# Sorting edges by source in a graph kernel: ranks from pairs of columns, a marked maximum, run sums turned afterwards, and the sort's preparation dealt out over the dense front

## The reference

```python
h = relu(layernorm(x))
feat = (h @ W).reshape(N, 2, 64); el, er = (feat*attn_l).sum(-1), (feat*attn_r).sum(-1)
e = leaky_relu(el[src] + er[dst]);  alpha = softmax of e over the edges of each dst
x = x + layernorm(segment_sum(feat[src]*alpha, dst) + bias)*gamma + beta
agg = h = relu(layernorm(x))
for _ in range(3):
    t = agg[dst]                                     # tail = dst, head = src
    att = ((agg[src] @ q_w) * tanh(rel * t @ k_w)).sum(1)
    w = softmax of att over the edges of each src
    agg = normalise(segment_sum(w * rel * t, src) / max(cnt, 1)); out += agg + h
```

## Time and profile before

| | |
|---|---|
| median of 3 runs | 9688.9 us (9686.51 to 9689.91) |
| the profiled execution | 9688.46 us, span 9686.6 us |
| mean granted clock of PE | 0.966 |
| front, from the first feature product to the first rank | 30.9 to 69.6 us |
| sort, first rank to last run sum | 69.6 to 778.9 us |
| start of the attention loop | about 850 us |

### The profile page before, as it was taken

One profiled execution on the slowest core, in us unless ns is written; L12 is line 12 of the kernel. 1 busy time (PEld: TensorE's weight loads), 2 busy tenths in 40 slices (PEclk: granted clock), 3 DMA queues, 4 the chain that ended last, 5 costly groups with the idle time before them and its releaser, 6 DMA issues.

```text
span 9686.6 us, 277606 instructions
## 1 busy us (share of the span) xinstructions
PE 8121.7 (84%) x65693; PEld 7065.2 (73%) x65693; DVE 7856.9 (81%) x33661; ACT 7227.1 (75%) x23594; POOL 6824.5 (70%) x7069
## 2 busy tenths in 40 slices
PE   7996777777775888888887888888887888888887
PEld 6985666666664777777776777777776777777776
DVE  7998999999997777777777777777776777777777
ACT  2204999999997777777776777777776777777777
POOL 1335777777775777777776777777776777777776
PEclk9998999999998999999998999999998999999998
DMA  2002444444444555555555555555555555555555
GB/s 53 5 12 77 109 107 109 107 109 109 109 108 115 158 159 160 157 157 158 160 159 163 158 159 160 157 157 159 160 158 162 158 159 160 158 157 158 160 159 146
DMA packets 1133287, 1309.57 MB, mean 135 GB/s; under 512 B 452805, under 2 KB 846875, under 8 KB 1132861
## 3 DMA queue, kind: packets, MB, share of 16 engines
q1 hardware_dynamic: 902182, 843.26, 28.5%
q0 software_dynamic: 229264, 460.98, 18.8%
q10 hardware_dynamic: 1670, 3.16, 0.1%
HBM read 1041.61 MB, written 261.38 MB: 135 GB/s over the span
## 4 chain that ended last, share of the span: by engine, by line
PE 35%; DMA 21%; issue 16%; DVE 11%; POOL 11%; ACT 3%; SPq 1%; DVEq 1%; POOLq 0%; ACTq 0%
PE bank L770 28%; DMA agg<-agg_d,arena 18%; POOL agg L732 11%; PE bank L930 2%; PE bank L915 2%; PE bank L883 2%; DMA agg<-feat_d,arena 2%; DVE arena L1709 2%; DVE agg L1610 2%; DVE agg L1600 2%; ACT arena L1045 1%; ACT arena L1125 1%; DVE arena L1686 1%; DVE arena L1590 1%; DVE arena L1684 1%
## 5 line engine op out<-in xcount | busy, mean ns | idle before, releaser
L732 POOL DMA_INDIRECT agg<-agg_d,arena x5124 | 4871.4, 951 | 1684.9 <-issue 1378.8
L1709 DVE TENSOR_TENSOR arena<-agg,bank 128x256 f32<-128x256 f32 x2562 | 1079.1, 421 | 1392.4 <-DMA agg<-agg_d,arena 1175.6
L770 PE MATMUL bank<-arena 128*128 128x129 f32 x10248 | 1760.4, 295 | 317.5 <-ACT arena L1125 294.1
L732 POOL DMA_INDIRECT agg<-feat_d,arena x1708 | 1618.0, 947 | 532.0 <-issue 410.1
L770 PEld LDWEIGHTS bank<-arena 128*128 128x128 f32 x10248 | 1377.5, 195 | 445.5 <-issue 435.2
L1121 ACT ACTIVATE arena<-arena 128x1 f32<-128x1 f32 x2562 | 755.1, 295 | 1167.9 <-DVE arena L1574 1146.6
L770 PE MATMUL bank<-tmp,wide 128*128 128x256 f32 x5124 | 1577.3, 391 | 4.8 <-DMA wide<-left_d 4.8
L770 PE MATMUL bank<-tmp,kw_s 128*128 128x256 f32 x5124 | 1567.0, 388 | 0.1
L930 PE MATMUL bank<-ident,arena 128*128 128x128 f32 x5124 | 1026.7, 283 | 508.4 <-DVE arena L1709 505.8
L930 PEld LDWEIGHTS bank<-ident,arena 128*128 128x128 f32 x5124 | 694.5, 144 | 931.7 <-DVE arena L1709 711.6
L1116 ACT ACTIVATE arena<-agg,arena 128x256 f32<-128x256 f32 x2562 | 1341.6, 524 | 16.8 <-DVE arena L1702 11.9
(11 more groups left out here) (244 smaller groups left out, 17334.3 us busy)
## 6 DMA issues: line engine op xcount, KB each, us to landing
state_d<-arena SPq DMA_DIRECT2D x488, 455.0 KB
arena<-key_d SPq DMA_DIRECT2D x489, 448.0 KB
arena<-type_d SPq DMA_DIRECT2D x367, 448.0 KB
wide<-left_d SPq DMA_DIRECT2D x2562, 64.0 KB
agg<-agg_d,arena POOLq DMA_INDIRECT x5124
agg<-feat_d,arena POOLq DMA_INDIRECT x1708
arena<-er_d SPq DMA_DIRECT2D x854, 1.0 KB
arena<-peers SPq DMA_DIRECT2D x489, 7.0 KB
```

The costliest lines, as they stand in the source:

```text
L732: nc.gpsimd.indirect_dma_start(out=rows_r[:, k % R, c, 0:width], out_offset=None, in_=table, in_offset=bass.IndirectOffsetOnAxis(ap=peer_r ...
L770: return nc.tensor.matmul(out, lhsT, rhs, start=start, stop=stop)
L1709: V.tensor_tensor(val_r[:, j % R, :, 0:F], rows_r[:, j % R, :, 0:F], bank[0][:, 0:G].rearrange("p (c f) -> p c f", c=2), ALU.mult).then_in ...
```

## The change

Seven edits, made together:

1. The seven passes and `spread(0)`, `carry(0)` are no longer ahead of the feature copies; `fields(t)` deals them out between the steps.
2. `couple` is the sum of `block_hot` over pairs of neighbouring columns (DVE, bf16, 6 x 49). Rank adds pairs instead of single columns; the column before an odd one is added by one matmul with a step of two.
3. Rank adds also 4096 on the own block (`mark16`, a diagonal). The slot is then the maximum over blocks, taken straight from the bank, and slot_hot compares with 4096 to 4159.
4. `gather_runs` has `slot_hot` as weights (64 columns) and both halves of `carried` (98 columns) moving, into 64 partitions; ACT copies the sums (`summed`) and PE transposes them a turn later (`turn_runs`), before ACT makes the run.
5. Three of 13 columns of `carried` are made by ACT (`carry_share`, six activations), the rest by DVE.
6. `run_at` has four places; DVE waits for the store of run n-4.
7. `er` is stored as node, block x head, and loaded from there.

```diff
-        er_d = dram("er_d", (NB, P, HEADS), F32)
+        er_d = dram("er_d", (P, NB * HEADS), F32)
...
-                            sp.dma_start(er_r[:, j % U, :], er_d[bass.ds(blk, 1)].rearrange("o p c -> p (o c)")).then_inc(q["block"][j % U], 16)
+                            sp.dma_start(er_r[:, j % U, :], er_d[:, bass.ds(blk * HEADS, HEADS)]).then_inc(q["block"][j % U], 16)
...
                     mm(to, before16[:], block_hot[:, h, lo:hi, :], True, False)
-                    for c in range(hi - 1):
-                        at = max(c + 1, lo)
-                        last = mm(to[:, at - lo:hi - lo, :], ones16[:], block_hot[:, h, c:c + 1, :].to_broadcast([P, hi - at, NB]),
-                                  False, c == hi - 2)
+                    mm(to, mark16[:], block_hot[:, h, lo:hi, :], False, False)
+                    n_odd = (hi // 2) - (lo // 2)
+                    first = 1 - lo % 2
+                    mm(to[:, first:first + 2 * n_odd - 1:2, :], ones16[:], block_hot[:, h, lo - 1 + first:lo - 1 + first + 2 * n_odd - 1:2, :], False, False)
+                    if half == 0:
+                        pe.wait_ge(couples_made, n + 1)
+                    for m in range(hi // 2):
+                        at = max(2 * m + 2, lo)
+                        if at < hi:
+                            last = mm(to[:, at - lo:hi - lo, :], ones16[:], couple[:, h, m:m + 1, :].to_broadcast([P, hi - at, NB]),
+                                      False, 2 * m + 4 > hi - 1)
...
                 pe.wait_ge(slots_made, n + 1)
+                pe.wait_ge(share_carried, n + 1)
                 if n >= 2:
                     pe.wait_ge(run_copied, n - 1)
-                for j in range(2):
-                    for c in range(SC):
-                        last = mm(bank[4 + h][0:NB, j * CAP:(j + 1) * CAP], carried[:, h, c, j, :], slot_hot[:, h, c, :], c == 0, c == SC - 1)
-                last.then_inc(run_summed, 1)
+                for c in range(SC):
+                    last = mm(bank[4 + h][0:CAP, 0:2 * NB], slot_hot[:, h, c, :], carried[:, h, c, :, :].rearrange("p j n -> p (j n)"), c == 0, c == SC - 1)
+                last.then_inc(run_summed, 1)
+
+            def turn_runs(n):
+                h = n % 2
+                pe.wait_ge(sum_copied, n + 1)
+                for j in range(2):
+                    last = nc.tensor.transpose(bank[4 + h][0:NB, TURN_AT + j * CAP:TURN_AT + (j + 1) * CAP], summed[:, h, j, :], ident[0:CAP, 0:CAP])
+                last.then_inc(run_turned, 1)
...
+            def carry_share(n):
+                h = n % 2
+                act.wait_ge(hot_made, n + 1)
+                if n >= 2:
+                    act.wait_ge(run_summed, n - 1)
+                for c in range(SHARE):
+                    for j in range(2):
+                        last = nc.scalar.activation(carried[:, h, c, j, :], block_hot[:, h, c, :], ACT.Identity,
+                                                    scale=payload[:, n * SC + c, j:j + 1], bias=nought[:, 0:1])
+                last.then_inc(share_carried, 1)
...
+            carry_share(0)
+            carry_share(1)
+            for n in range(CHUNKS):
+                act.wait_ge(run_summed, n + 1)
+                if n >= 2:
+                    act.wait_ge(run_turned, n - 1)
+                nc.scalar.copy(summed[:, n % 2, :, :].rearrange("p j n -> p (j n)"), bank[4 + n % 2][0:CAP, 0:2 * NB]).then_inc(sum_copied, 1)
+                if n >= 1:
+                    copy_run(n - 1)
+                if n + 2 < CHUNKS:
+                    carry_share(n + 2)
...
+            def couples(n):
+                h = n % 2
+                dve.wait_ge(hot_made, n + 1)
+                V.tensor_tensor(couple[:, h, :, :], block_hot[:, h, 0:SC - 1:2, :], block_hot[:, h, 1:SC:2, :], ALU.add).then_inc(couples_made, 1)
...
                 for half, (lo, hi) in enumerate(((0, HALF), (HALF, SC))):
-                    ranked_at = step(V.tensor_tensor(ranked[:, lo:hi, :], bank[2 * h + half][:, 0:(hi - lo) * NB].rearrange("p (c n) -> p c n", n=NB),
-                                                     block_hot[:, h, lo:hi, :], ALU.mult))
+                    slot_at = step(V.reduce_max(slot[:, lo:hi], bank[2 * h + half][:, 0:(hi - lo) * NB].rearrange("p (c n) -> p c n", n=NB), axis=AX))
                 if n + 1 < CHUNKS:
                     spread(n + 1)
-                dve.wait_ge(sort_step, ranked_at)
-                slot_at = step(V.reduce_sum(slot[:], ranked, axis=AX))
+                    couples(n + 1)
                 dve.wait_ge(run_sized, n + 1)
-                if n >= 2:
-                    dve.wait_ge(run_stored, 16 * (n - 1))
-                V.tensor_copy(run_at[:, h:h + 1], ends[:, n:n + 1])
+                if n >= 4:
+                    dve.wait_ge(run_stored, 16 * (n - 3))
+                V.tensor_copy(run_at[:, n % 4:n % 4 + 1], ends[:, n:n + 1])
```

More of the change, by code:

```diff
@@ L36 @@
 HALF = (SC + 1) // 2
+COUPLES = SC // 2
+MARK = 4096.0
+SHARE = 3
+TURN_AT = P
 VALID = 1 << 13
@@ L826, in _ @@
                     last.then_inc(feat_ready, 1)
-            for n in range(CHUNKS + 1):
+            for n in range(CHUNKS + 2):
                 if n < CHUNKS:
@@ L991, in _, with copy_run @@
                     nc.scalar.copy(batchT[:, (t - 1) % 2, 0:n], bank[(t - 1) % 2][:, 0:n]).then_inc(hiddenT_copied, 1)
[L993 to L994 removed]
+            def carry_share(n):
[8 more added lines that the diff above has]
+                last.then_inc(share_carried, 1)
+            def copy_run(n):
+                act.wait_ge(run_turned, n + 1)
                 if n >= 4:
```

76 lines of the change are left out of this document (52 added, 24 removed).

## The result

The changed kernel takes 9548.47 us, the median of 4 runs (9546.95 to 9554.53), against 9689.4 for the kernel before beside it (9686.51 to 9692.17): ratio 0.9856, 95% interval 0.9839 to 0.9873, that is 140.9 us less. The forecast was 9542, 146.6 less. The profiled execution is the one of 9554.53 us, span 9552.7.

What follows compares the result with a forecast made beforehand. The sort was taken as PE-bound, its turn falling from 5.51 to 4.35 us. Sort -139.5, after the last rank +1.1, front -8.2: total -146.6 from 9688.5, so 9542 us; range 9521 to 9590.

Steps and rivals of the forecast that it cites:

- Front: Dense front before the sort: passes dealt out between feature copies, rank 0 at 61.4 us, -8.2 us, range -7 to -10.
- rival (e): Run sums on TensorE: fp32 weight loads don't overlap, 3.85 us instead of 2.28, turn 5.9, +193 us, total 9735; chance 0.02.
- The transposes: TensorE in a sort turn: two new transposes of 64 columns, about 0.06 us each, 0.13 together.
- VectorE: VectorE's work in a sort turn without waits: 4.14 us after the change, with couples at 0.46; 4.72 before.
- Side jobs: VectorE's packing, beta and plans in the sort: cost beyond its slack 27 us (20 to 30), before 11.3.
- ScalarE: New load in a sort turn: six activations 1.9 us, plain turns 2.3, sign turns 4.0 to 4.2, hidden under 4.35.
- Rival (b): ScalarE bounds the 49 sign turns at 4.8 us instead of 4.35: +22 us, total 9564; chance 0.12.
- Stores: Start of the sort: VectorE's 13.34 us wait for the first run store goes; first store lands by 80 us.
- Rival (c): GpSimd's chain of run stores sets the turn: average landing 4.9 us, turn 5.2, +105 us, total 9647; chance 0.04.
- Tail: From the last rank to the first plan: 12.5 us instead of 11.4, +1.1 us.
- Rival (a): Sort: three engines close in length hold one another up, turn 4.7 us, +43 us, total 9585; chance 0.17.
- Rival (d): Attention loop: strided er loads hold it up; 0.175 us more per group eats the gain, 9690 or more; chance 0.02.

Runs made afterwards that it cites:

- e1: Changed kernel with edit 1 undone: fields, first spread, couples and carry ahead of the feature copies again; 13014.12 us, ratio 0.9899 to the kernel before.
- e2: Changed kernel with edit 4 undone: carried as weights, slots moving, no transposes; 13050.83 us, ratio 0.9925 to the kernel before.
- e3: Changed kernel with edit 2 undone: rank adds single columns, no couples; 13091.87 us, ratio 0.9959 to the kernel before.
- after: First profiled execution of the changed kernel, without further edit; 9554.53 us, against 9688.5 for the profiled kernel before.
- e7: Changed kernel with the transposes issued ahead of the run sums instead of behind them; 13004.06 us, ratio 0.9904 to the kernel before.
- e9: Changed kernel with edit 5 undone: ScalarE carries no columns, VectorE all thirteen; 13035.78 us, ratio 0.9906 to the kernel before.
- e5: Changed kernel again, no edit, as measure for the runs on its chip; 12994.45 us, ratio 0.9897 to the kernel before.
- e12: Changed kernel once more, no edit, on another chip; 13022.21 us, ratio 0.9896 to the kernel before.
- e10: Changed kernel with 4096 folded into the triangular matrix and sizes summed from six couples and the last column; 12992.14 us, ratio 0.9869 to the kernel before.
- e6: Changed kernel with edit 6 undone: two places for run positions, VectorE waits for store n-2; 13307.61 us, ratio 1.0134 to the kernel before.
- e8: Changed kernel with 4096 on the diagonal of the triangular matrix, no matmul with mark16; 12965.48 us, ratio 0.9879 to the kernel before.
- e4: Changed kernel with edit 7 undone: er stored in 8-byte pieces, loaded in one piece per block; 13022.31 us, ratio 0.9894 to the kernel before.
- e11: e10's kernel with ScalarE carrying five columns instead of three outside the sign turns; 12994.51 us, ratio 0.9866 to the kernel before.

## Why the prediction was right

The forecast was 6.5 us below the time (9542 for 9548.5), inside the range of 9521 to 9590, and the mechanism held at each place, with the transposes, VectorE's turn, its side jobs and the tail mis-sized. That the total came out so near is in part luck: by the landmarks, where 2 us can be told, the forecast gained 11.2 us too much (146.6 for 135.4). Step by step:

- **Front.** -8.2 forecast, -8.3 measured, and e1 takes 8.2 of it back. Step pace 1.53 for 1.52, rank 0 at 61.30 for 61.4.
- **Rank, sizes, run sums on TensorE.** 1.56, 0.37 and 2.28 forecast; 1.57, 0.36 and 2.32 measured. The weight loads of 64 columns stay under 98 moving ones, so rival (e) is out: with loads that don't overlap the turn would have been 5.9. e2 and e3 price the two edits by themselves: 0.50 and 0.79 us a turn.
- **The transposes, the term that was mis-sized.** The prediction took "0.06 each: 0.13". They take 0.24 to 0.25, in two positions (after, and e7). Of the 0.15 by which the turn of 4.50 exceeds 4.35, this is 0.11 and the run sums 0.04: 123 x 0.15 = 18.5 us over the 123 turns.
- **VectorE, mis-sized the other way.** 4.14 forecast, 4.02 measured. Couples start to start takes 0.24 for "0.46"; spread in front of it 0.84 for 0.73, since couples waits for it; the maxima from PSUM are no dearer than the products were, 0.79 for 0.80. The prediction priced couples at spread's rate. But 294 elements of carry, the three columns of edit 5, cost 0.31 by themselves (e9's 1.40 against 1.09), and the whole of couples, 294 elements too, takes 0.24, so it goes faster; spread, all 16-bit as well but with broadcast operands, takes 0.80 for 637. The Trainium skill, "VectorE: DVE Perf Modes", section "What auto-detection actually checks", gives a tensor_tensor whose tensors are all 16-bit with step 1 the double rate; this trace agrees for couples, with 0.24. Edit 3 took the reduction of 0.73 out of VectorE's turn. With it left in, the turn would be about 4.75 by VectorE and no longer 4.50 by TensorE, an estimate from 4.02 and 0.73 that no run tests.
- **Side jobs.** 27 us forecast, 18.6 measured: 571.2 is 123 x 4.50 - 0.9 + 18.6, and about 1 of the 18.6 is TensorE's clock in the first turns (75.8 us up to position 15, 74.8 in e5 and e12). The side jobs' work is as forecast, 39 us of busy time for 37, but the slack is 0.48 per turn and not 0.2, because both engines missed their forecasts in opposite directions. Turns 40 to 51 run at 4.62, 4.02 for the bare turn and 0.6 for beta. The two misses cancel in part: +18.5 - 8.4 leaves +10 in the sort.
- **ScalarE.** Six activations in 2.02 us, 0.32 us apart by their starts, for "1.9"; 4.05 in a sign turn, for "4.0 to 4.2". Rival (b) was to hold if one cost more than 0.35 us net. They take 0.32, and in the sign turns ScalarE still waits 0.45 of 4.50, so the rival is out. It stays out in e10, where TensorE's own turn is 4.07 and ScalarE's work in a sign turn just fits. The Trainium skill, "VectorE: DVE Perf Modes", section "The TRN2 errata — SBUF-src ops pay a fixed extra latency per instruction", warns of short instructions on ScalarE too; the rows bear it out (0.32 us for 49 elements, when 1612 take 1.62), but the three columns moved pay all the same, since ScalarE had the time: e9 is 15.7 us slower without.
- **Stores.** The 13.34 us are gone: the run positions of turns 2 to 4 wait for nothing. er's store lands in 14.6 us for 31.7, the first run store is issued at 77.03 (about 74 forecast) and the next, which waits for its landing ("by 80"), at 82.23; VectorE asks for it at 86.08 ("about 85"), so the margin was 4 us and not 5. Rival (c), the chain of landings, stays away with four places. What the prediction did not say is how near it is: it priced edit 6 by the first store alone, and e6 shows that without it nearly every turn waits, 2.6 us in the median, which makes the kernel slower than before. Its rival (c) had the right resource and the wrong condition: not the mean landing, but the distance between position and store.
- **Tail.** +1.1 forecast, +2.4 measured: 13.9 for 12.5. The first of the last two stores is issued 8.3 us after rank 123 starts (7.5 forecast), and the two take 5.6 (5.0 forecast).
- **Rival (a)**, that engines so close to each other hold one another up. A turn of 4.50 could have been read as half of it. It isn't: VectorE waits some 0.4 in each plain turn (0.1 to 0.3 forecast), TensorE for nobody, and in e10 three engines meet within 0.05 us without a loss in the plain turns. What closeness does cost is seen behind side jobs: there TensorE waits for VectorE, and in e8 and e10 its clock falls at five and eight places in the sort.
- **Rival (d)**, strided loads of er: 945 ns a gather of features for 944 before, 2145.6 us for the whole loop for 2143.7, and e4 with er in pieces is not faster.

In sum: front -8.3, sort -129.5, tail +2.4: -135.4 at the first plan, against -146.6 forecast. The medians differ by 140.9; the 5.5 us between are within what executions of one kernel differ by (9546.95 to 9554.53), and the profiled one is the slowest of the four.

## What to carry to other kernels

When several engines share a loop, write down the bare turn of each, then the side jobs by turn. An edit that shortens the longest engine pays in full only down to the second, and only in turns where the second has nothing else to do: here 0.27 us less on TensorE in each of 123 turns paid 16 us of 33, and another 10 came from moving VectorE's load in the turns that had side jobs. A faster TensorE also waits longer behind those turns, and its granted clock can fall there: about 5 of the missing 17 us. So look at the granted clock by stretches of a few us, and not at its mean over the stage (0.98 in e8's sort, 1.00 in e5's).

An edit that delays a result by a turn lengthens every circle that it is part of. Count, for each ring of buffers, how many turns lie between writing a place and the landing that frees it; the same two places that were nearly enough for runs stored at once cost 313 us with runs stored a turn and a copy later.

Short instructions between long ones are best priced by their start-to-start time, with neighbours of another kind on both sides: two transposes of 64 columns cost 0.24 us and not 2 x 0.06.

## What the runs showed of the hardware that was not expected

- **The two transposes.** 64 fp32 columns each, 0.24 to 0.25 us from the first of them to the next group, after the run sums and after the sizes alike. The run sums of before took 0.059 for 64 columns, so this is twice the time of the columns. Why stays open: a count of transposes (one or four) would have told a fixed part from a part for each, and that wasn't tried.
- **The store of er** occupies SyncE's queue for 9.87 us with 128 rows (10.84, 10.92 and 10.90 in e1, e5 and e12) and for 10.89 with 6272 pieces of 8 bytes (10.08 in e4): the form makes no difference to the issue. It does to the landing, 14.6 to 15.9 us with rows, 31.7 and 34.0 with pieces. What sets the time of the issue is not settled.
- **TensorE's granted clock** falls after waits of 1 us and more, and not in every execution. At the start of the sort, in the windows of after, 60 to 65 us is at 0.73 and 65 to 70 at 0.59, so most of it at the lower level of 1.2 GHz:

```profile
60.00:65.00 5.00, 2.74 (x28) 2.05 (x28) 3.02 (x8) 1.04 (x4) 0.00 (x0) 0.73 0.45 130
65.00:70.00 5.00, 4.91 (x42) 3.89 (x43) 4.30 (x10) 2.02 (x6) 0.00 (x0) 0.59 1.20 279
70.00:75.00 5.00, 5.00 (x66) 4.52 (x65) 4.80 (x8) 2.15 (x7) 0.00 (x0) 1.00 1.18 261
```

  TensorE had waited 2.44 us before 61.30 and 1.06 before 65.09. e12 and e5, the same kernel with the same first wait, show 1.00 in all three windows, while e6, e8, e9, e10 and e11 show 0.50 to 0.57 between 65 and 70. One fall costs about a microsecond (after takes 75.8 us up to position 15, e5 and e12 74.8). In the changed kernel at most one such fall is seen in an execution (none in e5); where TensorE is shorter and waits longer for VectorE it adds up, to 5.3 us in e8 and 6.6 in e10. Which wait brings the clock down isn't settled: e5 stayed at 1.00 behind 1.99 us, e8 fell behind 1.16.
- **Chips that differ in the loops alone.** The span of the sort is 569.7 us in after and 568.9 and 570.3 in e5 and e12, on two other chips. The attention loop takes 2145.6 us in after and 2862.3 in e12, and from there to the end it is 6708 and 9449. Why isn't known from these runs.
